# Softplus and dt by channel group inside the scan of a vision-Mamba block, and u turned once per image

## The reference

```python
xs = ...                      # u: silu(conv(x)), flat and transposed image, each forward and reversed
dts, Bs, Cs = split(einsum(xs, x_proj_w))
dts = softplus(einsum(dts, dt_projs_w) + dt_projs_b)
As  = -exp(A_logs)
# per token t, for each channel and each of 16 states
h = h * exp(d_t * As) + (d_t * u_t) * B_t
y = sum_n(h * C_t) + D * u_t
```

## Time and profile before

| | |
|---|---|
| median of 3 runs | 1658.44 us |
| lowest, highest | 1650.5, 1660.56 us |
| profiled execution, span from first to last instruction | 1655.7 us |
| share of the span busy: TensorE, VectorE, ScalarE, GpSimd | 82%, 74%, 61%, 62% |
| scan stage, first to last scan instruction | 189.5 to 1348.2 us |
| mean granted TensorE clock | 0.947 |

### The profile page before, as it was taken

One profiled execution on the slowest core, in us unless ns is written; L12 is line 12 of the kernel. 1 busy time (PEld: TensorE's weight loads), 2 busy tenths in 40 slices (PEclk: granted clock), 3 DMA queues, 4 the chain that ended last, 5 costly groups with the idle time before them and its releaser, 6 DMA issues. The chain is left out here.

```text
span 1655.7 us, 66567 instructions
## 1 busy us (share of the span) xinstructions
PE 1352.8 (82%) x30504; PEld 835.7 (50%) x30504; DVE 1229.4 (74%) x1025; ACT 1015.1 (61%) x1916; POOL 1026.3 (62%) x294
## 2 busy tenths in 40 slices
PE   7997779787886978788697878869787868879998
PEld 6734546444553645455364445545454524436555
DVE  4875298979898897989889797988979884742220
ACT  2458678766877876677777767777776540402222
POOL 0002189889898988979898888979888960000000
PEclk7898789999999999999999999999999997889999
DMA  8244424323233432323343231334323234101101
GB/s 323 109 163 171 120 67 109 96 66 96 67 90 75 107 96 66 96 67 87 76 108 89 72 99 55 90 73 109 92 71 99 78 99 177 38 0 39 39 35 43
DMA packets 73479, 151.09 MB, mean 91 GB/s; under 512 B 33238, under 2 KB 41942, under 8 KB 72816
## 3 DMA queue, kind: packets, MB, share of 16 engines
q1 hardware_dynamic: 73200, 146.83, 30.4%
HBM read 101.72 MB, written 32.51 MB: 81 GB/s over the span
## 5 line engine op out<-in xcount | busy, mean ns | idle before, releaser
L1193 POOL TENSOR_TENSOR s_h<-s_h,s_crow 128x2048 f32<-128x2048 f32 (+1 forms) x256 | 880.4, 3469 | 197.4 <-DVE s_h L1158 197.3
L1158 DVE TENSOR_TENSOR_SCAN s_h<-s_a,s_pb 128x1024 f32<-128x1024 f32 x384 | 864.2, 2277 | 183.1 <-PE s_py L1041 78.1
L1002 PE MATMUL s_pb<-k_area,m_dtut 64*64 64x64 f32 x24576 | 466.8, 224 | 196.0 <-DVE s_h L1158 163.0
L1002 PEld LDWEIGHTS s_pb<-k_area,m_dtut 64*64 64x64 f32 x24576 | 421.0, 137 | 387.5 <-DVE s_h L1158 233.1
L1041 PE MATMUL s_py<-s_h,k_eye 64*64 64x512 f32 x3072 | 416.6, 599 | 21.2 <-ACT y_y L1090 15.6
L284 ACT ACTIVATE k_area<-k_mask,m_bt 128x64 f32<-128x64 f32 x992 | 273.9, 337 | 0.0
L1084 ACT ACTIVATE s_a<-y_y,m_aneg 128x1024 f32<-128x1024 f32 x192 | 218.6, 1140 | 38.1 <-DVE s_h L1158 38.1
L1084 ACT ACTIVATE s_a<-m_dup,m_aneg 128x1024 f32<-128x1024 f32 x192 | 219.4, 1143 | 31.1 <-DVE s_h L1158 31.1
L199 POOL TENSOR_TENSOR k_area<-m_bt,k_mask 128x2048 f32<-128x2048 f32 x33 | 145.6, 4412 | 130.0 <-ACT m_bt L262 130.0
L1041 PEld LDWEIGHTS s_py<-s_h,k_eye 64*64 64x64 f32 x3072 | 89.9, 136 | 34.2 <-ACT y_y L1090 16.0
L262 ACT COPY y_y<-m_pm 128x384 f32<-128x384 f32 (+1 forms) x96 | 49.2, 513 | 90.4 <-PE m_pm L219 78.2
(11 more groups left out here) (189 smaller groups left out, 1260.5 us busy)
## 6 DMA issues: line engine op xcount, KB each, us to landing
s_crow<-scratch_xd SPq DMA_DIRECT2D x256, 256.0 KB, 4.0
k_area<-in_x_dram SPq DMA_DIRECT2D x4, 1536.0 KB, 7.8
scratch_xt<-y_y SPq DMA_DIRECT2D x4, 1536.0 KB, 10.1
y_y<-y_y SPq DMA_DIRECT2D x24, 256.0 KB, 3.4
m_dup<-m_dup SPq DMA_DIRECT2D x24, 256.0 KB, 3.2
out_dram<-t_out SPq DMA_DIRECT2D x32, 192.0 KB, 1.9
k_area<-scratch_xt SPq DMA_DIRECT2D x3, 1536.0 KB, 6.8
scratch_xd<-h_dbl SPq DMA_DIRECT2D x8, 512.0 KB, 2.6
```

Of the source, the lines that this page charges most:

```text
L1002: mm = pe.matmul(pb[par * HALF:(par + 1) * HALF, step % 2, r * BANK + blk:(r + 1) * BANK:BLK], dtut[here, u % 2, blk, g * HALF:(g + 1) * H ...
L1158: nc.vector.tensor_tensor_scan(h[:, step % (TRIPLES * CG), f], a[:, step % RING, f], pb[:, step % 2, f], 0.0, ALU.mult, ALU.add).then_inc( ...
L1193: nc.gpsimd.tensor_tensor(here, here, c.unsqueeze(1).broadcast_to([P, groups.stop - groups.start, L]), ALU.mult).then_inc(hc_ready, 1)
```

## The change

- Softplus works by channel group (64 channels of all 1024 tokens: 8 runs of 64 columns), not by third of the tokens. Logarithms come at steps 6, 10, 14; the four VectorE operations of a group behind the scans of steps 7 and 8, 11 and 12, 15 and 16.
- `times_u` becomes three instructions of 512 columns, behind the scans of steps 9, 13, 17.
- DUP becomes 6 chunks of 4 transposes of 128 x 64, at steps 9, 10, 13, 14, 17, 18. Each pair waits on TensorE for its group's softplus.
- u is turned once per image: UT for the flat orientation at steps 19, 21, 23 of unit 2 (of each image) and step 5 of unit 3; the result is stored to DRAM at the next image's first unit and loaded in transposed order, for the other orientation, at its second. The forms `ub` are gone from the head (L714, L717 and 12 stores), and UT reads u with a step of 8 columns.
- `build_d` moves from behind triples 1 and 4 to behind triples 2 and 5; `exponent` comes one step earlier; the rows of B are spread anew.
- The DMAs of the scan are placed anew: rows at n = 3, u at n = 4 once per image, each group's doubling by itself.

```diff
+SLOTS = {0: ("Z", 0), 1: ("Z", 1), 2: ("Z", 2), 3: ("Z", 3), 4: ("BT", 0), 9: ("DUP", 0), 10: ("DUP", 1),
+         13: ("DUP", 2), 14: ("DUP", 3), 17: ("DUP", 4), 18: ("DUP", 5)}
+LN_AT = (6, 10, 14)
+UT_AT = (19, 21, 23)
+def chunk_at(u, i):
+    if i == 5 and u % 4 == 3 and u + 1 < UNITS:
+        return u + 1, "UT", 3
+    if i in UT_AT and u % 4 == 2 and u + 2 < UNITS:
+        return u + 2, "UT", UT_AT.index(i)
+    if i in SLOTS and u + 1 < UNITS:
+        return u + 1, *SLOTS[i]
+    return None
...
+    def store_ut(self, sp, d, b):
+        sp.wait_ge(self.chunk_taken, CHUNK[4 * b, "UT", 3] + 1)
+        sp.dma_start(d["ut"][b].rearrange("(p k) c -> p k c", k=BLK), self.ut[:]).then_inc(self.ut_out, 16)
+    def turn_ut(self, sp, d, b):
+        sp.wait_ge(self.ut_out, 16 * (b + 1))
+        sp.wait_ge(self.dtu_ready, CG * (4 * b + 2))
+        for q in range(4):
+            src = d["ut"][b].rearrange("(q k w) c -> q w k c", q=4, k=BLK)[q]
+            sp.dma_start(self.ut[q::4], src).then_inc(self.ut_in, 16)
...
-                mm = pe.transpose(pm[:, lh * DI:lh * DI + P], tokens(u01[:], 2 * i + lh), eye[:])
+                mm = pe.transpose(pm[:, lh * DI:lh * DI + P], u01[:, 2 * i + lh::BLK], eye[:])
         if what == "DUP":
-            pe.wait_ge(self.dt_ready, ROUNDS * (u + 1))
-            r, chans = i % 2, slice(0, P) if i < 2 else slice(P, DI)
-            here = slice(r * HALF, (r + 1) * HALF)
-            for blk in range(BLK):
-                mm = pe.transpose(pm[0:chans.stop - chans.start, blk::BLK], self.dt_of[here, blk, chans], eye[here, here])
+            g, h = i // 2, i % 2
+            pe.wait_ge(self.dt_ready, ROUNDS * u + g + 1)
+            for at in range(BLK // 2):
+                mm = pe.transpose(pm[0:HALF, at::BLK // 2], self.dt_of[:, h * BLK // 2 + at, g * HALF:(g + 1) * HALF], eye[:])
...
-    def times_u(self, dve, u):
+    def times_u(self, dve, u, g):
+        dve.wait_ge(self.dt_ready, ROUNDS * u + g + 1)
...
+        here = slice(g * HALF, (g + 1) * HALF)
+        self.nc.vector.tensor_tensor(self.dtut[:, u % 2, :, here], self.dt_of[:, :, here], self.ut[:, :, here],
                                      ALU.mult).then_inc(self.dtu_ready, 1)
... (head)
-                nc.scalar.activation(xb[0].rearrange("p (k j) -> p k j", k=BLK), by_block(acc[:, kind]),
-                                     ACT.Silu, bias=bias).then_inc(xb_ready, 1)
-                nc.scalar.activation(turned_to(xb[1]), turned_from(acc[:, kind]), ACT.Silu, bias=bias).then_inc(xb_ready, 1)
...
             m.chunk(pe, 0, "DUP", 0)
+            m.chunk(pe, 0, "DUP", 1)
             x_proj(1, (2, 3))
-            m.build_rows(act, 0, 2, 0, 2 * BLK)
+            m.build_rows(act, 0, 2, 0, 3 * BLK)
... (scan, VectorE)
-                        if 9 <= i < 15:
-                            softplus(u + 1, (i - 9) // 2, (i - 9) % 2 * 2)
-                            softplus(u + 1, (i - 9) // 2, (i - 9) % 2 * 2 + 1)
-                        if i == 15:
-                            m.times_u(dve, u + 1)
+                        for g, at in enumerate(LN_AT):
+                            if i in (at + 1, at + 2):
+                                softplus(u + 1, g, 2 * (i - at - 1))
+                                softplus(u + 1, g, 2 * (i - at - 1) + 1)
+                            if i == at + 3:
+                                m.times_u(dve, u + 1, g)
... (scan, GpSimd)
-                    if n == 1:
+                    if n == 2:
                         m.build_d(pool, nc.gpsimd.tensor_tensor, u, 3)
-                    if n == 4 and u + 1 < UNITS:
+                    if n == 5 and u + 1 < UNITS:
                         m.build_d(pool, nc.gpsimd.tensor_tensor, u + 1, 1)
```

More of the change, by code:

```diff
@@ L73, in unit_of, with group @@
     return u // 4, u // 2 % 2, u % 2
[L76 to L81, removed]
+SLOTS = {0: ("Z", 0), 1: ("Z", 1), 2: ("Z", 2), 3: ("Z", 3), 4: ("BT", 0), 9: ("DUP", 0), 10: ("DUP", 1),
[10 more added lines that the diff above has]
+    return None
 CHUNK = {}
+for _what in [("Z", ch) for ch in range(4)] + [("BT", 0)] + [("UT", ch) for ch in range(4)] + [("DUP", i) for i in range(2 * CG)]:
+    CHUNK[(0, *_what)] = len(CHUNK)
 for _u in range(UNITS):
[L86 to L97, removed]
+    for _i in range(STEPS):
+        if chunk_at(_u, _i):
+            CHUNK[chunk_at(_u, _i)] = len(CHUNK)
 def by_block(t):
     return t.rearrange("p (j k) -> p k j", k=BLK)
+def group(t, g):
+    return t.rearrange("p (k c) -> p k c", k=BLK)[:, :, g * HALF:(g + 1) * HALF]
 def turned_from(t):
@@ L224, in chunk @@
         if what == "UT":
[L225 removed]
+            pe.wait_ge(self.shared["u_in"], 16 * 3 * (b + 1))
             for lh in range(2):
@@ L522, in _ @@
             store_xd(0, 0)
-            sp.wait_ge(ub_out[0], 16 * 2)
-            load_u(sp, d, keep, shared, 0, "flat")
+            sp.wait_ge(u_out, 16 * 2)
+            load_u(sp, d, keep, shared, 0)
             sp.wait_ge(xd_out[0], 16)
@@ L537, in _ @@
             store_xd(1, 3)
-            m.double(sp, 0, range(CG))
+            for g in range(CG):
+                m.double(sp, 0, g)
             store_z(1, TT // 2, TT)
@@ L879, in _ @@
             nc.vector.scalar_tensor_tensor(zs, zs, 0.0, lnz, ALU.max, ALU.add).then_inc(m.dt_ready, ROUNDS)
-            m.times_u(dve, 0)
+            for g in range(CG):
+                m.times_u(dve, 0, g)
         @block.gpsimd
@@ L1049, in _ @@
                         add_y((step - LAG) // CG, (step - LAG) % CG)
-                    if u + 1 < UNITS:
-                        for what in chunks_of(u + 1):
-                            if chunk_slot(*what) == i:
-                                m.chunk(pe, u + 1, *what)
-                    elif 6 <= i < 6 + TT:
+                    if chunk_at(u, i):
+                        m.chunk(pe, *chunk_at(u, i))
+                    if u == LAST_U and 6 <= i < 6 + TT:
                         t = i - 6
@@ L1124, in _, with softplus @@
         def _(dve):
-            def softplus(u, r, part):
-                at = round_cols(r)
-                count = ROUNDS * u + r + 1
+            def softplus(u, g, part):
+                t, z, e = group(pm[:], 0), group(zs, g), group(ez, g)
+                count = ROUNDS * u + g + 1
                 if part == 0:
```

148 lines of the change are left out of this document (65 added, 83 removed).

## The result

The kernel after the change takes 1667.94 us (median of 20 runs, 1659.89 to 1678.21), the kernel before 1655.11 (20 runs): a ratio of 1.0064, 95% interval 1.0045 to 1.0083. So by the ratios the change costs 11 to 12 us (13 by the medians); I had forecast 1655 us, 3 us less than before.

A forecast was written before the change was run, and what follows sets the result against it. VectorE, running the scans, was held by waits for TensorE. Gains of 53 us less costs of 50 gave 3 us under 1655.7, so 1652.7; with the median 2.7 above, 1655. Range 1612 to 1688; the forecast's own, 1642 to 1670.

The forecast's parts named there:

- (h): TensorE waits for dt at each group's first DUP chunk; claimed hidden with 0.2 to 1.1 us to spare.
- DUP holds TensorE: Rival: the cover of DUP's wait missed by 0.5 us at three places, 22 us, 1677; no separate chance given.
- (k): Third `times_u`, behind scan 17, waits 1.27 us for GpSimd's triple 5 in all 15 units: 19 us cost.
- (l): First `times_u`, behind scan 9, waits 2.7 us for `build_d` in seven units with late scan 8: 19 us cost.
- (e): Scan 8 of units 4, 8, 12 waits 5.26 us for ScalarE; claimed 3 us gained each, 9 us.
- The race: VectorE's `times_u` starts 0.04 us before `build_d`; rival that it loses in eight units: 29 us, 1684, chance 0.25.
- (i): `times_u` split into three of 0.69 us against one of 1.73: 0.34 x 15 = 5 us cost.
- (g): UT at its new steps on TensorE costs 7.5 us; its stepped read of u, bounds 0 and 12, put at 0.
- (a): UT leaves steps 5 to 8 of the seven odd units; VectorE's waits at steps 6, 8, 9 shrink: 22 us gain.
- (b): DUP leaves steps 16 to 19; waits behind it go: 7 us gain, bounds 0 and 10.
- (c): Waits about step 0 shrink as the DMAs of doublings, rows and u are set apart: 7 us gain, of 0 to 14.
- (f): In the head, two extra silu per kind go: 3 us gain, between 0 and 6.

The follow-up runs named there:

- e1: The kernel after the change, with DUP, two of the logarithms and UT moved one step later (UT to 20, 22, 23); ratio 0.9816 to the kernel before.
- e2: The kernel after the change, with the matmuls of `spread_b` issued twice at steps 9, 13 and 17; ratio 0.9953 to the kernel before.
- e3: The kernel after the change, with GpSimd multiplying the fifth triple as one group and then two; ratio 1.0027 to the kernel before.
- e7: e1 with `build_d`'s fourth piece put between the third triple's two instructions in even units from 2 on; ratio 0.9766 to the kernel before.
- e6: e1 with the edit of e3 (fifth triple cut as one group and two); ratio 0.9864 to the kernel before.
- e5: e1 with the edits of both e3 and e7; ratio 0.9820 to the kernel before.

## Why the prediction was wrong

**Step (h) failed**, "Hidden with 0.2 to 1.1 us to spare". The wait itself was worked out rightly: TensorE there at 2.1 and dt at 4.8, 2.7 us, measured 2.89 in unit 3 (and less where TensorE comes late: 107 us over 45, 2.4 on average). Then I let `spread_b` and `add_y` take the 2.0 us that they take in a row without a wait. They took 3.1 and 3.6 us in the first two groups of unit 3, because TensorE, having stood 2.9 us, came back at 1.2 GHz. Against a cover of 0.2 to 1.1 us that opens waits of VectorE at steps 10, 11, 15 and 18. Priced at nothing, it shows as 32 us of such waits and cost 36 to 41 us in all (e1), 18 or more of them by the clock (e2). I had the rival, "DUP holds TensorE", but priced it at 0.5 us in each of three places (22 us; measured 0.35, 1.4 and 0.4) with a chance inside other cases, and had no clock in it. Of the prediction's own signs of being wrong, one is what the trace shows: waits of VectorE at scans 10, 14 or 18 for TensorE.

**(k), third product.** The wait is 1.13 us, in all 15 units, for 1.27 foretold. What failed is that I put all of it on the path: in place it cost 6 to 7 us of 19, as TensorE was late behind it anyway (e3). **(l), first product.** 2.53 us in four units and 2.71 in one rather than 2.7 in seven; units 4 and 12 were spared because scan 8 no longer waits there, see (e). 12.8 us for 19; taking it away gave 8 to 11 (e7). The race was won in the other ten units by 0.01 to 0.05 us, the same margin as before. **(i)**: 3 x 0.67 for 1.73 is 0.28 a unit, 4 us for 5.

The rule that these items rest on, from the Trainium skill, page "SBUF — State Buffer", section "Who interferes with whom", holds here: the product waits until the GpSimd instruction that began first has ended (3.20), and where it began first GpSimd waits (`build_d` 4.1 us for 3.62). Of a queue of GpSimd's instructions the section says nothing; e6 shows that a waiting VectorE may be passed by the next (5.48).

**(g), UT.** The waits at the new places are near what I gave: at step 6 of units 3, 7 and 11 2.25 us, where I had left 1.73, and about the start of unit 3 0.26 + 0.33 + 1.87 = 2.5. The stepped read, at 0 in my sum with bounds of 0 and 12, is 0.53 us a chunk and 1 to 18 us of time; I took the low end, while ScalarE's row of 2.15 against 1.14 pointed to the other. The same page of the Trainium skill, section "Door 1: The DMA port swizzle", says that SBUF has lines of 16 bytes, that each access that crosses to a new line pays, and that the free stride therefore ends at four fp32 columns. The step here is eight, the rows agree that it costs, and I hadn't weighed it.

**Gains**, by VectorE's waits ahead of each step's scan, before and after. (a) 22.9 us for 22: steps 8 and 9 of the odd units have no waits, and step 6 is at 0.46 in the four units. (b) Steps 19 to 22 fell by 4.7, UT's new waits included, where 7 less 2 of UT was forecast. (c) Nothing for 7: in the eleven units from 1 on without UT in front, the waits at step 0 add up to 4.8 before and 6.2 after, and those at steps 1 and 2 of all units fell by 1.5, so the DMAs that now stand apart bought next to nothing. (d) `carry`'s wait fell from 6.03 to 4.60, 1.43 for 1.31. (e) ScalarE's waits of 5.26, 4.99 and 5.25 at step 8 fell to 0, 0.71 and 0, 14.8 us for 9. Waits of 0.46 and up at steps 8 and 9 that no term had are gone too, 4.8. (f) 5.1 for 3 in one pair of executions, 1 to 6 by the scatter of the head.

The whole stage adds up. VectorE's instructions follow one another in the trace, so the stage is what it does and what it waits. The products take 31.4 us more (as far as nothing else of VectorE overlaps them) for the 43 of (i), (k) and (l). The waits at steps 10, 11, 14, 15 and 18 went from 2.2 to 32.0. All its other waits fell by 48.5, for 43 forecast with (g). The rest is 0.6 longer: 31.4 + 29.8 - 48.5 + 0.6 = 13.3, by which the stage grew. These are places, not prices: e3 shows that a wait taken away in one place can come back in the next.

That the sum, 1655, still came within 13 us of 1668 is therefore partly luck: some 30 us of waits that I had at nothing stand against products 12 cheaper and other waits 6 better than forecast.

## What to carry to other kernels

When an edit makes an engine wait in the midst of its queue, price what stands behind the wait at the clock that it will have there, not at the speed of the row; look for another step where the datum is long ready (here one step later was worth 2.5%). A wait that one engine imposes has its full price only where no other wait follows it: look at the next idle entry of the same engine first. An instruction order that holds by 0.01 to 0.05 us is a cost waiting to be triggered, by the cure of something else too.

## What the runs showed of the hardware

In unit 3 a wait of TensorE of 2.9 us was followed by about 4 us at a granted clock of 0.59 on average (1.2 GHz for most of it), in e2 one of 1.6 us by 1.00. In the kernel after this befell 26 of 29 waits of over 2.6 us and 3 of 16 shorter ones (0.92, 1.96 and 2.08 us), so the length of the wait alone doesn't decide. 64 more matmuls ahead of each wait (45 waits) made the whole 18 us faster. A chunk of ten matmuls that read fp32 columns eight apart took 1.74 us for 1.21; in units 1 to 14 the weight loads of its 64 x 64 matmuls took 206 ns for 133 and the matmuls 278 for 224. And a VectorE instruction that waited for GpSimd let a second GpSimd instruction pass in 11 of 12 cases of e5 and e6 (up to 5.52 us for one of 0.67), but in none of the 15 of the kernel after.
